# Passage from a mixer phase to an attention phase: work regrouped on both sides of the barrier

## What is computed

```python
qkv = x @ Wqkv + bqkv                       # 16 heads of 16
xn = x / max(norm(x, per head), 1e-12)      # for q and k
proj = einsum('bhtd,rhdm->rbhtm', xn, omega)
s = quad_nodes
arg = clip(proj * sqrt(2 s) - s, -20, 20)
feat = exp(arg) / sqrt(M) * sqrt(quad_weights)
# causal, in chunks of 128: running sums of k-features times v, and of k-features
out = (q_feat . kv_state) / max(q_feat . k_state, 1e-6)
x = layernorm(x + out @ Wout + bout)
```

## Time and profile before

| | |
|---|---|
| median of 3 executions | 1445.27 us (1445.09 to 1446.31) |
| profiled execution | 1448.13 us, span 1446.5 us |
| PE busy | 1371.3 us (95%) |
| DVE busy | 914.3 us (63%) |
| ACT busy | 684.4 us (47%) |
| POOL busy | 551.6 us (38%) |
| mean granted clock of PE | 0.976 of full |
| PE busy, 310 to 320 us | 6.37 us of 10 |
| PE busy, 320 to 330 us | 6.37 us of 10, granted clock 0.50 |
| PE busy, 330 to 340 us | 9.09 us of 10, granted clock 0.68 |

### The profile page before, as it was taken

The page is one execution under the profiler, slowest core; times in us unless marked ns, Lnnn a source line. Parts: engine busy times, 40 slices in busy tenths (PEclk is TensorE's granted clock), DMA queues, the critical chain, the costliest instruction groups (busy, mean ns, idle before and its releaser), DMA issues. The chain is left out here.

```text
span 1446.5 us, 33923 instructions
## 1 busy us (share of the span) xinstructions
PE 1371.3 (95%) x12256; PEld 1190.8 (82%) x12256; DVE 914.3 (63%) x1944; ACT 684.4 (47%) x1257; POOL 551.6 (38%) x503
## 2 busy tenths in 40 slices
PE   6989999989999999999998999999999999999994
PEld 5778888877677777777777988888899999999984
DVE  4666767676776877877774464444555555555547
ACT  2356667544545455445444433223355555555533
POOL 0144555442254354454310006422344444444421
PEclk9799999998999999999999999999999999999997
DMA  6333333105133133233115204633788888888885
GB/s 223 128 136 123 111 133 128 52 15 181 45 100 120 57 117 123 65 131 102 45 60 219 104 30 162 263 111 122 188 227 233 234 233 234 233 234 234 248 258 213
DMA packets 103869, 216.12 MB, mean 149 GB/s; under 512 B 18544, under 2 KB 74224, under 8 KB 96624
## 3 DMA queue, kind: packets, MB, share of 16 engines
q1 hardware_dynamic: 79552, 159.87, 33.8%
q0 software_dynamic: 23088, 54.31, 13.1%
q10 hardware_dynamic: 1152, 0.93, 0.2%
HBM read 150.23 MB, written 64.84 MB: 149 GB/s over the span
## 5 line engine op out<-in xcount | busy, mean ns | idle before, releaser
L2637 PE MATMUL ps<-e_xhl,s_whl 128*128 128x256 f32 x1848 | 245.7, 282 | 0.0
L2637 PEld LDWEIGHTS ps<-e_xhl,s_whl 128*128 128x128 f32 x1848 | 231.0, 189 | 0.2 <-issue 0.2
L2019 PE MATMUL ps<-s_xhl,s_whl 128*128 128x512 f32 x660 | 164.5, 398 | 1.4 <-PEq L1108 1.4
L2468 POOL DMA_INDIRECT xs<-e_y,e_slot_id x78 | 122.1, 1566 | 90.5 <-ACT e_y L2502 71.4
L492 POOL TENSOR_TENSOR b_hhl<-b_h,b_hhl 128x512 fp32r<-128x512 f32 x64 | 94.7, 1482 | 139.7 <-ACT b_hhl L756 118.3
L2019 PEld LDWEIGHTS ps<-s_xhl,s_whl 128*128 128x128 f32 x660 | 122.1, 190 | 26.5 <-issue 1.8
L2616 PE MATMUL ps<-s_whl,e_ghl 128*128 128x256 f32 x936 | 139.3, 285 | 0.6 <-issue 0.6
L2716 DVE TENSOR_TENSOR e_g<-ps,e_act_h 128x256 f32<-128x256 f32 x156 | 66.2, 424 | 112.8 <-ACT e_act_h L2515 112.8
L2616 PEld LDWEIGHTS ps<-s_whl,e_ghl 128*128 128x128 f32 x936 | 121.8, 189 | 0.8 <-issue 0.7
L589 PE MATMUL ps<-b_w,b_hhl 128*128 128x256 f32 x768 | 105.3, 287 | 6.3 <-DVE b_turned_rows L862 5.6
L2515 ACT ACTIVATE e_act_h<-ps 128x256 f32<-128x256 f32 x156 | 60.1, 385 | 107.9 <-PE ps L2637 102.4
(11 more groups left out here) (384 smaller groups left out, 2737.2 us busy)
## 6 DMA issues: line engine op xcount, KB each, us to landing
s_whl<-wlo SPq DMA_DIRECT2D x38, 1024.0 KB, 5.0
s_whl<-wlo SPq DMA_DIRECT2D x38, 512.0 KB, 3.7
c_eraw<-in_expert_w POOLq DMA_DIRECT2D x24, 512.0 KB, 4.9
wlo<-c_elo POOLq DMA_DIRECT2D x24, 512.0 KB, 3.0
wall<-in_expert_w SPq DMA_DIRECT2D x8, 1536.0 KB, 9.2
xg<-b_zeros POOLq DMA_DIRECT2D x13, 780.0 KB, 3.9
e_xr<-xg SPq DMA_DIRECT2D x39, 260.0 KB, 3.8
x<-rows_out SPq DMA_DIRECT2D x16, 512.0 KB, 3.2
```

Source lines behind the costliest of these rows:

```text
L2019: mm = pe.matmul(ps[:, H + 2 * (m % 2) + w, :], whl[:, wp, e, lo:lo + P], xhl[:, k, xp, kd, :], start=q == 0, stop=q == 3 * KD - 1)
L2468: gp.indirect_dma_start(xs, bass.IndirectOffsetOnAxis(ap=slot_id[:, i, b:b + 1], axis=0), y[:, k, b, :], None, compute_op=ALU.add).then_in ...
L2637: mm = pe.matmul(ps[:, H + m, w * SLOT:(w + 1) * SLOT], whl[:, k, wp, lo:lo + P], xhl[:, k, xp, kd, :], start=q == 0, stop=q == 3 * KD - 1)
```

## The change

In the mixer's tail, the normed rows, their turning and their halves are taken out on POOL, PE, ACT and DVE. POOL's two squares move from behind tiles 4 and 5 to behind tiles 2 and 3. On DVE, all four projections and omega's scaling now stand ahead of the scales, and omega's low half ahead of the norms; ACT's high half of omega moves from tile 7 to tile 4. ACT takes one exponential of one column (into UNIT, which nothing reads) as its last work of the phase. SP loads the next step's rows of x there.

```diff
                     sp.dma_start(omr, flat(omega)).then_inc(s["omega_in"], 16)
+                    sp.wait_ge(s["ft_done"], KD)
+                    sp.dma_start(x0[:], x2[1]).then_inc(x0_in, 16)
...
-            def next_normed():
-                gp.wait_ge(s["next_root"], 1)
-                for c in range(KD):
-                    heads_of = lambda ap: ap.rearrange("p b (s c h d) -> p (b s) c h d", s=2, c=KD, d=HD)[:, :, c]
-                    gp.tensor_tensor(heads_of(ahead.sq[:]), heads_of(ahead.qk[:]),
-                                     ahead.nrm[:, 1, :].rearrange("p (m c h) -> p m c h", c=KD, h=HEADS1 // KD)[:, :, c].unsqueeze(3).to_broadcast(
-                                         [P, 2 * BATCH, HEADS1 // KD, HD]), ALU.mult).then_inc(s["next_qn"], 1)
...
-                    if is_(i, STEPS) and m in (4, 5):
-                        next_squares(m - 4)
-                    if is_(i, STEPS) and m == MT - 1:
-                        next_normed()
+                    if is_(i, STEPS) and m in (2, 3):
+                        next_squares(m - 2)
...
-                if is_(i, STEPS + 1):
-                    for c in range(2):
-                        turn_normed(c)
...
-                    if is_(i, STEPS) and m == MT - 1:
+                    if is_(i, STEPS) and m == 4:
                         act.wait_ge(s["omega_scaled"], 1)
                         act.activation(flat(om[:, 0]), omr, ACT.Copy).then_inc(s["omega_hi"], 1)
...
                     act.wait_ge(s["amp_ready"], 1)
                     act.activation(fc[:, LNA], fc[:, QBIAS], ACT.Ln).then_inc(s["ln_done"], 1)
-                    for c in range(2):
-                        act.wait_ge(s["fn_done"], c + 1)
-                        act.activation(ahead.qkt[:, 0, 2 * c, :], ps[:, FN_BANK[c], :], ACT.Copy).then_inc(s["fn_hi"], 1)
+                    act.activation(fc[:, UNIT], fc[:, KBIAS], ACT.Exp)
...
                 if is_(i, STEPS + 1):
-                    omega_low()
                     ve.wait_ge(s["ln_done"], 1)
                     pre.link(ve.tensor_tensor(fc[:, QBIAS], fc[:, LNA], fc[:, KBIAS], ALU.add))
                     ve.tensor_tensor(fc[:, QBIAS], fc[:, QBIAS], fc[:, NONE], ALU.add)
                     fed(STEPS - 1, k)
-                    for c in range(2):
-                        next_normed_low(c)
                     return
...
                 row_stats(ch, BATCH, N)
+                if is_(i, STEPS):
+                    for b in range(4):
+                        next_projected(b)
+                    scale_omega()
                 if not has_ssd(i):
                     ve.wait_ge(s["x1_ready"], STEPS)
                 scales(ch)
...
                 if is_(i, STEPS):
-                    for b in range(2):
-                        next_projected(b)
-                    scale_omega()
-                    for b in range(2, 4):
-                        next_projected(b)
+                    omega_low()
                     next_norms()
```

```diff
+        FIRST_OF_X = {0: ((Z_, "FV", 0), (Z_, "FV", 1), (Z_, "FT", 0), (Z_, "FT", 1), (Z_, "FM", 0), (Z_, "FM", 1),
+                          (A_, "FN", 1), (B_, "FN", 3), (C_, "FQ", 0)),
+                      1: ((A_, "FQ", 1), (B_, "FQ", 2)),
+                      2: ((A_, "FQ", 3),),
+                      3: (), 4: (),
+                      5: ((C_, "BO", 0),),
+                      6: ((A_, "BO", 1),),
+                      7: ((A_, "FN", 0), (B_, "FN", 2))}
+        HI = ("FT", "FN", "FM", "BC")
...
-            sp.dma_start(xr[:], x2[1]).then_inc(s["x_in"], 16)
...
+
+            def normed(c):
+                heads = lambda ap: ap.rearrange("p b (s c h d) -> p (b s) c h d", s=2, c=KD, d=HD)[:, :, c]
+                return gp.tensor_tensor(heads(sq[:]), heads(qk[:]),
+                                        nrm[:, 1, :].rearrange("p (m c h) -> p m c h", c=KD, h=HEADS1 // KD)[:, :, c].unsqueeze(3).to_broadcast(
+                                            [P, 2 * BATCH, HEADS1 // KD, HD]), ALU.mult)
...
             prime(gp, [elo_ready])
+            for c in range(KD):
+                normed(c).then_inc(s["first_qn"], 1)
             gp.memset(three_halves[:], 1.5).then_inc(s["const_set"], 1)
             gp.wait_ge(s["const_set"], 1)
             for k in range(2):
                 gp.dma_start(eraw[:, k], ew[:, k * EC:(k + 1) * EC]).then_inc(eraw_in[k], 16)
-            gp.memset(va[:], 0.0).then_inc(s["cleared"], 1)
-            gp.wait_ge(s["cleared"], 1)
-            gp.memset(va[:, :, :, HD:HD + 1], 1.0).then_inc(s["cleared"], 1)
-            gp.memset(state[:], 0.0).then_inc(s["cleared"], 1)
...
-                        pe.wait_ge(s["x_in"], 16 * step)
+                        if isinstance(i, int) and i == 0:
+                            pe.wait_ge(x0_in, 32)
+                        else:
+                            pe.wait_ge(s["x_in"], 16 * i)
...
+                elif name == "FM":
+                    pe.wait_ge(s["first_qn"], 1)
+                    for b in range(BATCH):
+                        mm = pe.transpose(ps[:, xp, b * P:(b + 1) * P], sq[:, b, 2 * a * P:(2 * a + 1) * P], ids[:])
...
             def body(i):
                 for t in range(PAIRS):
+                    x_steps(i, t, Z_)
                     if pair(i, t, 0) is not None:
                         features(i, t)
                     x_steps(i, t, A_)
...
+            ve.memset(va[:], 0.0).then_inc(s["cleared"], 1)
+            ve.memset(state[:], 0.0).then_inc(s["cleared"], 1)
+            ve.wait_ge(s["cleared"], 1)
+            ve.memset(va[:, :, :, HD:HD + 1], 1.0).then_inc(s["cleared"], 1)
             body(0)
```

68 lines of the change are left out of this document (30 added, 38 removed).

## The result

The changed kernel takes 1449.17 us, the median of 9 executions (1447.96 to 1454.67); the kernel before took 1445.09 us beside it on the same chip (9 executions, 1442.86 to 1446.84). The medians differ by 4.1 us. The ratio estimated from all executions is 1.0036, with a 95% interval from 1.0023 to 1.0048, which is 5.2 us (3.3 to 6.9). The forecast was 1446.0, within what cannot be told from no change.

The account below looks back on a forecast made before the run. PE was taken as the bound, busy 95% of the span, with 13.4 us of idle and low clock to win from. Terms -2.2 + 10.6 - 2.4 - 5.9 + 0.6, applied to the 1445.27 median, gave 1446.0 us; range 1440.5 to 1450.0.

Parts of the forecast that it names:

- start of attention: At the barrier behind the mixer: attention starts on PE at 323.4 instead of 325.60, 2.2 us earlier.
- from there to the first features: Behind the barrier: values, turned rows and first turnings now precede the first features, at 334.0; adds 10.6 us.
- first to third features, against before: Early attention phase: this way takes 10.3 us instead of 12.7, a gain of 2.4 us.
- third features to the next step's first: Behind the third features: two turnings and three projections are already done, taking out 5.9 us.
- turnings and first projection at low clock: Around the first features: part of this PE work runs at low clock, adding 0.6 us.
- From the first to the third features: Early attention phase: features, turnings, one wait, projections, scores and keys at full clock take 10.3 us; third features at 344.3.
- slower rival: Behind the barrier: values do not bring the clock back, low until dense projections; 1448.5 us, up to 1450; 25%.
- What is then already done: Behind the third features: two turnings and three projections that stood there before are gone, 5.9 us of PE work.
- last sign of being wrong: Behind the third features: new gaps appearing there would show the forecast wrong; no size given.
- barrier term: Mixer's end: late scales, POOL waits and norms summed on DVE; attention starts at 323.4, 2.2 us earlier.
- The rival in which the tail is not held up: Mixer's tail: DVE and POOL interleave more kindly, scales ready by about 306; gain 3.5 to 6.5 us, about 1440.5; 17%.
- The chain up to the first features: Behind the barrier: 5.3 us of low-clock values, then turnings, copies and low halves, 5.3 us; 10.6 us in all.

Follow-up runs that it names:

- the run with later roots: Changed kernel with the previous rows' root chain moved behind the next pair's mask and ACT's scalings one pair later; ratio 1.0015 (0.9999 to 1.0031) to the kernel before.
- the order with split values: Changed kernel with values split around the first turnings, turned x and projections behind the first features; ratio 1.0020 (1.0007 to 1.0033) to the kernel before.
- the kept-busy run: Changed kernel with 22 unused matmuls, 11 behind the down-projections and 11 in the chain's gaps; ratio 0.9997 (0.9986 to 1.0009) to the kernel before.
- the old tail: Changed kernel with the mixer tail's order on DVE, POOL and ACT as before; ratio 1.0019 (1.0008 to 1.0031) to the kernel before.

## Why the prediction was wrong

Each term of the sum, counted on the passage:

| term of the sum | predicted | measured |
|---|---|---|
| start of attention | -2.2 | -3.56 |
| from there to the first features | +10.6 | +10.30 |
| first to third features, against before | -2.4 | +1.48 |
| third features to the next step's first | -5.9 | -4.16 |
| turnings and first projection at low clock | +0.6 | counted above |
| sum | +0.7 | +4.06 |

**The step that failed is "From the first to the third features ... After, at full clock".** The forecast took the clock to be up for good once dense values had brought it back; the only low piece allowed for was 0.6 us. The trace shows it up at 326 and down again at 332.8, after 2.52 us of idle time in the four gaps of the chain that the same text had worked out (a turning, a copy, a low half, twice). The run with 11 matmuls in that chain, whose clock holds there, goes from the first to the third features in 10.18 us: the 10.3 of the forecast. So the groups and waits of the term were right, and what failed is its clock; the 3.95 us that this run gives back are the term's error of 3.9, or 3.3 beyond the 0.6 allowed. The slower rival came out nearest in size (1448.5, at 25%), but not by its mechanism either: it had the clock stay low behind the barrier for want of dense work, and decided by "below 1.00 at the first features". At the first features the clock was 1.00, so by its own sign this rival did not come about. Its sum is also wrong as it stands: 334.6, 10.3 for the way and its four additions (3.9) give 348.8 for the third features, not 347.4; measured were 346.5 in the time of the kernel before (47.50 + 298.99).

**The second error is "What is then already done", 5.9 us.** The work did move (two turnings, three projections), but only 4.16 us came back, because DVE and ACT had things to do under it. The forecast named one later gap as staying (1.06 us at 365.73) and did not ask what else that PE work hid. The forecast's own last sign of being wrong, new gaps behind the third features, came true: 0.32 at 356.98 and 0.33 at 366.58, where the kernel before has none up to 365.73. One piece of the missing 1.7 us is shown, the root chain ahead of the clip, about 1.1; the other 0.7 stays open.

**The barrier term was right in direction and too small**, -2.2 for -3.56. Its chain of steps is seen: DVE held whole POOL instructions long, ACT's write starting behind the scales, one PE gap (predicted 2.2, measured 1.47), a table load hidden. But the pieces were summed too high: the scales came 0.7 us sooner than the forecast's 310.7 (308.8, plus the 1.19 us by which this execution runs ahead, is 310.0), and the norms, which lost 2.0 in two waits at their beginning (1.23 for L1003 and 1.22 for L84 behind it, for 0.23 each), were done another 0.4 sooner than reckoned, the evacuation behind them another 0.2. The rival in which the tail is not held up is excluded by the 1.86 and 1.18 us of L943 and L946.

**The chain up to the first features held** (10.6 for 10.30), low clock in the values included: 5.38 us for 5.3. The memsets did not wait for POOL, as taken: 1.76 us for the 2048 columns, as at the program's start.

The error is thus 3.9 in one term (0.6 of it allowed for), 1.7 in another, and 1.4 and 0.3 the other way. That 1449.17 lies within the stated range is luck: the slower rival had opened the range that far, and its mechanism did not occur.

## What to carry to other kernels

A phase's opening chain of small steps that pass from engine to engine is judged by what it leaves PE idle, added up over the chain and not by its longest gap: at half clock, what stands behind it pays. Dense work put in front of such a chain did not keep the clock up through it; a few matmuls of no use in its gaps did (though 25 of them in the kernel before did not hold it throughout). Values split into the gaps held it there as well, but it fell later, behind the work that this had moved. Follow the clock to the end of the passage, in every run: a low stretch that one execution has and another has not (0.7 us in the run with later roots) can hide what an edit is worth. Work moved off a stretch in which other engines are busy gives back only what those engines do not then hold up: list what they do under it before booking its weight as a gain.

## What the runs showed of the hardware

**The clock can fall behind short gaps.** In the changed kernel no gap of the chain is over 1.41 us, and four of them, 0.35, 0.41, 0.35 and 1.41, in the 4.5 us up to 331.15, were followed by the fall at 332.8, although PE was busy from 331.15 on. With gaps of 0.18, 0.25 and 0.33 in that place it held. In the order with split values, gaps of 1.04, 0.42 and 1.42 in the 6.8 us up to 336.87 did not bring it down either, while 1.80 and 0.31 up to 354.81 were followed by a fall. The same gaps can go either way: 0.33 and 1.39 up to 368.61 in the changed kernel were followed by none, 0.33 and 1.39 up to 363.96 in the kept-busy run by one. The Trainium skill, TensorE: Matmul & The Clock Gate, "A second HAM failure mode: psum-queue depth-cycling", tells of a kernel in which short idle times between groups let the clock swing; the trace agrees, with 3.95 us as its price here. How the clock decides between these cases the runs do not show.

**The way back is unequally long.** The values brought the clock back behind five busy slices (321 to 325); in the second stretch PE was busy for eight (335 to 342, projections and features) before it rose. With the old tail the same values brought it back behind three (321 to 323).

**Small DVE operations were held for the whole of a POOL instruction, its memsets were not.** 8 columns took 1.86 us behind POOL's squares and 128 columns 1.23 behind a low half. This is the exclusive lock of which the Trainium skill, SBUF — State Buffer, "SBUF: two separate sides", speaks; the trace agrees also for one-input operations such as L946 (1.18 for 0.16). It works both ways: POOL's second squares took 2.87 us instead of 1.90 beside DVE's L978. And where DVE only clears memory, neither waits: the two memsets (1.76 and 0.91) ran at full rate beside POOL's two normed multiplications, and these took 3.83 us, against 4.74 in the kernel before, where DVE's L1004 with two inputs (to 318.19) still ran as they began at 317.13.
